# Weighted sums of the values, issued in pairs: six of the eighteen steps carry them in place of twelve

## The chip, the cores and the metric

The kernel runs on one core of a Trainium2 chip. The metric is the device time of one execution in microseconds (us), median of three runs. PE is TensorE, DVE VectorE, ACT ScalarE, POOL GpSimd, SP SyncE; PEld stands for TensorE's weight loads.

## The reference

For x of shape (4, 1024, 128), float32: a latent attention with 16 heads, a residual sum and a layer norm, a feed-forward block on weights and activations that are quantised to FP4 in blocks of 16, a residual sum and a second layer norm.

```
k_eff = (W_dq.T @ W_uq.T @ W_uk) per head;  v_eff = (W_uv.T @ W_o.T) per head
c_kv = x @ W_dkv.T;  q = x @ W_dq.T @ W_uq.T
attn = softmax(causal(q @ k_eff @ c_kv.T / sqrt(8)))
y = attn @ c_kv @ v_eff
x = layernorm(x + y)
gate, up = fp4_linear(x, w_gate), fp4_linear(x, w_up)
x = layernorm(x + fp4_linear(silu(gate) * up, w_down))
```

## The kernel before

The batch elements (4) are worked one after the other, the heads of each in four quads of four heads. A quad takes 18 steps (`STEPS`), a batch element 72 (`BODY`). In a step, PE issues in this order:

- `score_max` (L487, mask L490) for a tile 24 steps ahead: scores of which DVE takes row maxima (`maximum`, L750)
- the jobs due at this step (`misc_job`): transposes and projections in the bank `misc`, among them `yn` (L443, transposes of the attention output), `mt` (L438, the transposed maxima), and for the batch element before this one `gate` and `up` (L457), `ht` (L463), `down` (L472)
- `score_probs` (L504, mask L508) for this step's tile: transposed scores less the maxima, which ACT turns into probabilities (`exps`, L675), written to `probs`, six buffers in turn
- the calls of `weigh` (L524) due at this step

A call of `weigh` multiplies 128 keys of one half of the queries by the values: for each of the four heads an accumulating float32 matmul with a 128 x 32 weight block and 128, 256, 384 or 512 columns of `probs`, each head on its own 32 columns of the array, all into the bank `yt_ps`. The profile shows two matmuls for each, so eight a call. A quad has 12 calls (`W_LIST`, numbered 0 to 11; 0 to 3 are for the first half of the queries, 4 to 11 for the second). Their columns are 512, 384, 128, 256, then five times 512, then 384, 128, 256. The last tile that each needs is of step 1, 3, 3, 4, 6, 8, 10, 12, 14, 16, 16, 17. `W_STEP` gives the step in whose end PE issues each; a step of 18 or 19 is step 0 or 1 of the next quad.

Scores lie in three double banks `ring`, taken in turn by `score_max` and `score_probs`. So `score_probs` of a step waits for the maximum of the step before, and `score_max` for the exponentials of two steps before:

```
pe.wait_ge(t_exp.sem, pn + 1)                           # ahead of score_max
...
pe.wait_ge(s_max.sem, b * BODY + n + STEPS + LEAD)      # ahead of score_probs
```

ACT copies `yt_ps` out (`out_copy`, L683) after the exponentials of step 7 (first half) and of step 1 of the next quad (second half). DVE does in each step the maximum, then what is due: `combine` of the maxima (L759, after tile 17, in step 11), `output` (L783, L787) of a `yn` job, and pieces of the feed-forward block and of the norms. After `combine`, POOL splits the maxima in five operations (`top_split`, L986 to L994) for the job `mt` at step 13. POOL also multiplies, divides and rounds for the quantisation (L1058, L1063, L1027 to L1031). Each engine works strictly in its written order.

The feed-forward block of a batch element is worked during the attention of the next one, so quads 0 to 3 have none of it; after the last quad a closing stage does it alone.

Of the kernel before, what the change touches and what calls it, by code (L numbers as in the profile page):

```python
# [40 lines left out]
def build(nc, x, w_dq, w_uq, w_dkv, w_uk, w_uv, w_o, w_gate, w_up, w_down, out):  # L41
# [35 lines left out]
            W_LIST.append((max(t for t, _ in where.values()), c, j, where))  # L77
    W_LIST.sort(key=lambda w: w[0])
    WS = len(W_LIST)
    W_STEP = [3, 5, 6, 7, 9, 10, 12, 14, 16, 17, 18, 19]  # L80
    assert len(W_STEP) == WS and all(at > w[0] for at, w in zip(W_STEP, W_LIST))

    FREED = [max(n + 1 for n, w in enumerate(W_LIST) if t in [x for x, _ in w[3].values()]) for t in range(STEPS)]
# [50 lines left out]
    with ExitStack() as ctx:  # L134
# [259 lines left out]
        def _(pe):  # L394
# [164 lines left out]
            for b in range(B + 1):  # L559
# [3 lines left out]
                for n in range(BODY):  # L563
# [20 lines left out]

                    for w, at in enumerate(W_STEP):
                        g = n - at
# [534 lines left out]
```

## Time and profile before

| | us |
|---|---|
| median of three runs | 787.44 |
| the three runs | 787.44, 789.64, 785.46 |
| span of the profiled execution | 785.6 |

The profiled execution is known by its span, from its first to its last instruction; no other time of it is given. The profile page lists busy time by engine, a chain of work that ended last, and groups of instructions by line. The trace answers queries on a stretch of time: a timeline, the waits, and windows with the busy time of each engine. Stage by stage: the attention and feed-forward of the batch elements fill 110 to 690 us, before it lie preparation and the first maxima, after it the closing stage.

### The profile page before, as it was taken

The numbers are of one execution on the slowest core, as the hardware profiler recorded it, in microseconds if no ns is written. First come the engines' busy times: TensorE is split into PE (matmuls) and PEld (weight loads), VectorE is DVE, ScalarE is ACT, GpSimd is POOL, SyncE is SP. The second block draws the span as 40 slices with busy tenths as digits, with TensorE's granted clock in tenths as the row PEclk, the third lists the DMA queues.
The fourth block names the chain that finished last, engine by engine and source line by source line (L and its number), as shares of the span: only waits on it lengthen the run. The fifth ranks groups of instructions, "written<-read, shape, count | busy, mean of one in ns | idle before, by whom it ended". The sixth has DMA issues, their size and how long they took to land.

```text
span 785.6 us, 13071 instructions
## 1 busy us (share of the span) xinstructions
PE 661.5 (84%) x4839; PEld 328.1 (42%) x4839; DVE 589.9 (75%) x1053; ACT 393.2 (50%) x558; POOL 279.7 (36%) x402
## 2 busy tenths in 40 slices
PE   5197999999998989899898899899988997982523
PEld 2154444534443535444444445354434462441313
DVE  1287567677887979988798799978889797167871
ACT  2211566566575556565465566564656555751210
POOL 3700031000315543432236342524143344345752
PEclk9655899999999999999999999999999999995565
DMA  3462012302211032020401221011100000000000
GB/s 98 144 131 74 1 43 74 90 2 61 61 43 39 17 103 62 15 62 15 102 15 41 68 55 43 27 49 42 49 15 1 2 2 16 1 14 0 1 13 13
DMA packets 31073, 33.55 MB, mean 43 GB/s; under 512 B 5299, under 2 KB 18675, under 8 KB 31011
## 3 DMA queue, kind: packets, MB, share of 16 engines
q1 hardware_dynamic: 30099, 32.19, 14.6%
q8 instruction: 38, 0.62, 0.3%
q10 hardware_dynamic: 912, 0.54, 0.3%
q14 instruction: 24, 0.20, 0.1%
HBM read 23.84 MB, written 8.39 MB: 41 GB/s over the span
## 4 chain that ended last, share of the span: by engine, by line
PE 57%; DVE 22%; POOL 11%; issue 6%; ACT 1%; SPq 1%; DMA 1%; POOLq 0%; DVEq 0%; ACTq 0%
PE yt_ps L524 14%; PE ring L487 13%; PE ring L504 11%; DVE top L750 11%; PE ring L490 3%; PE ring L508 3%; PE misc L472 3%; PE misc L457 2%; DVE eg L860 2%; POOL hx L1029 2%; POOL hx L1027 2%; PE misc L443 1%; POOL hx L1031 1%; DVE z L817 1%; DVE hc L880 1%
## 5 line engine op out<-in xcount | busy, mean ns | idle before, releaser
L750 DVE TENSOR_REDUCE top<-ring 128x2 f32<-128x1024 f32 (+3 forms) x384 | 350.6, 941 | 101.8 <-PE ring L490 72.7
L675 ACT ACTIVATE probs<-ring 128x1024 f32<-128x1024 f32 x288 | 294.3, 1025 | 176.4 <-PE ring L508 110.9
L487 PE MATMUL ring<-k_op,q_op 72*128 72x512 bf16 (+3 forms) x768 | 209.7, 350 | 19.4 <-DMA q_op<-scratch_q 17.1
L504 PE MATMUL ring<-q_op,k_op 75*128 75x512 bf16 (+3 forms) x768 | 197.7, 332 | 13.8 <-DVE top L750 12.8
L524 PE MATMUL yt_ps<-probs,v_op 128*32 128x512 f32 (+3 forms) x1536 | 168.4, 511 | 0.3 <-ACT probs L675 0.3
L487 PEld LDWEIGHTS ring<-k_op,q_op 72*128 72x128 bf16 x768 | 69.8, 103 | 162.3 <-issue 109.8
L504 PEld LDWEIGHTS ring<-q_op,k_op 75*128 75x128 bf16 x768 | 73.3, 99 | 86.2 <-DVE top L750 35.0
L490 PE MATMUL ring<-mask_q,ident 128*128 128x128 bf16 x512 | 107.0, 230 | 0.0
L508 PE MATMUL ring<-mask_k,ident 128*128 128x128 bf16 x512 | 96.8, 224 | 0.0
L1050 POOL TENSOR_TENSOR r<-r,yq 128x128 f32<-128x128 f32 x32 | 14.5, 454 | 203.5 <-DVE yq L787 203.5
L860 DVE RECIPROCAL eg<-eg 128x118 f32<-128x118 f32 (+1 forms) x96 | 83.0, 867 | 0.0
L524 PEld LDWEIGHTS yt_ps<-probs,v_op 128*32 128x32 f32 x1536 | 30.5, 109 | 60.8 <-issue 46.3
L508 PEld LDWEIGHTS ring<-mask_k,ident 128*128 128x128 bf16 x512 | 51.4, 100 | 8.7 <-issue 5.1
L490 PEld LDWEIGHTS ring<-mask_q,ident 128*128 128x128 bf16 x512 | 53.2, 104 | 2.0
L1027 POOL TENSOR_TENSOR hx<-hx,hc 128x352 f32<-128x352 f32 x32 | 29.7, 928 | 41.8 <-DVE hc L883 41.8
L463 PE MATMUL ring<-ident,hx 128*128 128x128 f32 (+1 forms) x24 | 6.3, 394 | 34.4 <-POOL hx L1031 34.4
L986 POOL TENSOR_SCALAR top_parts<-top_all 128x32 bf16<-128x32 f32 x16 | 4.8, 297 | 76.9 <-DVE top_all L759 76.8
L1058 POOL TENSOR_TENSOR h<-gu,eg 128x352 f32<-128x352 f32 x32 | 29.6, 926 | 6.5 <-DVE eg L860 6.5
L1029 POOL TENSOR_TENSOR hx<-hx,hc 128x352 f32<-128x352 f32 x32 | 29.8, 930 | 2.5
L656 ACT ACTIVATE eg<-misc 128x352 f32<-128x352 f32 x24 | 11.1, 464 | 35.2 <-PE misc L457 35.2
L1063 POOL TENSOR_TENSOR hx<-h,h_inv 128x352 f32<-128x352 f32 x32 | 25.1, 785 | 8.9 <-DVE h_inv L875 8.7
L866 DVE TENSOR_REDUCE h_amax<-h 128x22 f32<-128x352 f32 x32 | 16.1, 504 | 14.7 <-POOL h L1058 14.6
(156 smaller groups left out, 706.1 us busy)
## 6 DMA issues: line engine op xcount, KB each, us to landing
k_op<-scratch_k SPq DMA_DIRECT2D x48, 192.0 KB
q_op<-scratch_q SPq DMA_DIRECT2D x144, 64.0 KB
scratch_q<-part SPq DMA_DIRECT2D x12, 256.0 KB, 2.4
scratch_k<-part SPq DMA_DIRECT2D x12, 256.0 KB, 2.4
xp<-in_L_attn_x_dram SPq DMA_DIRECT2D x4, 512.0 KB, 4.7
r<-in_L_attn_x_dram SPq DMA_DIRECT2D x8, 256.0 KB, 2.8
out_dram<-z SPq DMA_DIRECT2D x8, 256.0 KB, 2.3
q_op<-top_t SPq DMA_DIRECT2D x48, 8.0 KB, 1.9
```

The lines of the kernel that those rows point to most:

```text
L487: last = nc.tensor.matmul(ring[slot][:, e, at:at + n], q_op[0:ROWS, head, i * P:(i + 1) * P], k_op[0:ROWS, head, kc * CHUNK:kc * CHUNK + n ...
L490: last = nc.tensor.matmul(ring[slot][:, e, at + n - P:at + n], ident16[:, :], mask_q[:, :], start=False, stop=True)
L504: last = nc.tensor.matmul(ring[slot][:, e, at:at + n], k_op[0:rows, head, j * P:(j + 1) * P], q_op[0:rows, head, (c + 1) * CHUNK - n:(c + ...
L508: last = nc.tensor.matmul(ring[slot][:, e, at:at + P], ident16[:, :], mask_k[:, :], start=False, stop=True)
L524: last = nc.tensor.matmul(yt_ps[32 * q:32 * (q + 1), lo:CHUNK], v_op[:, j, 4 * a + q, :], probs[:, (STEPS * a + tile) % P_RING, q % 2, at: ...
L675: nc.scalar.activation(probs[:, n % P_RING, :, :], ring[(2 * n + 1) % 3][:, :, :], ACT.Exp, scale=SCALE).then_inc(t_exp.sem, 1)
L750: last = nc.vector.tensor_reduce(top[:, kc, p, :, i], ring[slot][:, :, at:at + n], AX.X, ALU.max)
L860: nc.vector.reciprocal(piece, piece).then_inc(s_v.sem, 1)
L1027: nc.gpsimd.tensor_tensor(dst, dst, magic, ALU.add).then_inc(s1.sem, 1)
L1029: nc.gpsimd.tensor_tensor(dst, dst, magic, ALU.subtract).then_inc(s2.sem, 1)
L1058: nc.gpsimd.tensor_tensor(hn.rearrange("p n k -> p (n k)"), gu[:, n, :], eg[:, n, :], ALU.mult).then_inc(h_p.sem, 1)
L1063: nc.gpsimd.tensor_tensor(hxn, hn, h_inv[:, n, :].unsqueeze(2).to_broadcast(sh), ALU.mult).then_inc(hd_p.sem, 1)
```

## The change

Only the steps of the calls move. Each call with an even number goes to the step of the call behind it, so that the calls lie two and two at steps 5, 7, 10, 14, 17 and 19.

```
-    W_STEP = [3, 5, 6, 7, 9, 10, 12, 14, 16, 17, 18, 19]
+    W_STEP = [5, 5, 7, 7, 10, 10, 14, 14, 17, 17, 19, 19]
```

## Rows read from the trace of the kernel before

**Rows 1.** The page, busy us of each engine (share of the span) x instructions.
```profile
PE 661.5 (84%) x4839; PEld 328.1 (42%) x4839; DVE 589.9 (75%) x1053; ACT 393.2 (50%) x558; POOL 279.7 (36%) x402
```

**Rows 2.** The page's groups: form, count, busy, mean ns, idle before and its releaser.
```profile
L524 PE MATMUL yt_ps<-probs,v_op 128*32 128x512 f32 (+3 forms) x1536 | 168.4, 511 | 0.3 <-ACT probs L675 0.3
```

**Rows 3.** The waits of PEld, 110 to 690 us: total us, times, longest.
```profile
PEld ring L504 <- DVE top L750: 34.2, 56, 2.2
```

**Rows 4.** Windows of quads 2, 6, 4 and 8; columns are in the first line.
```profile
core 0: us, PE busy (x) PEld busy (x) DVE busy (x) ACT busy (x) POOL busy (x), PEclk, DMA share, GB/s
146.26:179.06 32.80, 32.13 (x268) 14.33 (x265) 23.36 (x30) 19.65 (x21) 2.60 (x8) 1.00 0.13 38
299.33:340.00 40.67, 38.09 (x308) 19.70 (x306) 37.95 (x73) 23.27 (x33) 16.00 (x25) 1.00 0.13 37
212.19:254.27 42.08, 39.26 (x296) 18.52 (x293) 33.95 (x62) 25.52 (x35) 16.39 (x23) 1.00 0.13 37
376.69:423.78 47.09, 42.55 (x295) 19.42 (x293) 37.77 (x68) 25.66 (x35) 16.85 (x24) 0.93 0.24 62
```

**Rows 5.** Timeline of PE around a call (start, us), then L524 by source line.
```profile
306.81 0.22 PE L508 MATMUL ring<-mask_k,ident 128*128 128x128 bf16 x1
306.96 1.06 PE L524 MATMUL yt_ps<-probs,v_op 128*32 128x512 f32 x8
307.96 0.23 PE L487 MATMUL ring<-k_op,q_op 72*128 72x128 bf16 x1
...
L524 PEld LDWEIGHTS yt_ps<-probs,v_op x8: 106/108/109, 307.0 to 307.0; 128*32 128x32 f32 x8
L524 PE MATMUL yt_ps<-probs,v_op x8: 592/605/617, 307.0 to 307.4; 128*32 128x512 f32 x8
```

**Rows 6.** Timeline of steps 6 and 7 of quad 2.
```profile
158.12 0.61 PE L487 MATMUL ring<-k_op,q_op 72*128 72x512 bf16 x2
...
158.76 1.23 DVE L750 TENSOR_REDUCE top<-ring 128x2 f32<-128x1024 f32 x1 [0.66 <-PE ring L487]
...
159.08 0.43 PE L524 MATMUL yt_ps<-probs,v_op 128*32 128x128 f32 x8
...
160.04 0.61 PE L504 MATMUL ring<-q_op,k_op 75*128 75x512 bf16 x2
```

**Rows 7.** Windows of quad 2 by stretch: from step 2, 6, 8, 11, 15, 0.
```profile
150.55:158.12 7.57, 7.55 (x75) 4.33 (x71) 5.76 (x9) 4.79 (x6) 0.79 (x2) 1.00 0.36 106
158.12:161.15 3.03, 3.03 (x29) 0.85 (x25) 2.29 (x2) 1.83 (x3) 0.00 (x0) 1.00 0.00 0
161.15:166.82 5.67, 5.66 (x42) 2.08 (x39) 4.26 (x7) 3.97 (x5) 0.45 (x1) 1.00 0.01 3
166.82:174.28 7.46, 7.03 (x57) 2.97 (x53) 5.22 (x7) 4.36 (x6) 1.36 (x5) 1.00 0.02 3
174.28:179.99 5.71, 5.50 (x50) 2.50 (x47) 3.58 (x3) 2.86 (x4) 0.00 (x0) 1.00 0.01 3
179.99:183.35 3.36, 3.36 (x39) 1.60 (x35) 2.25 (x3) 1.84 (x3) 0.00 (x0) 1.00 0.47 135
```

**Rows 8.** Timeline of quad 2, DVE's combine and the last of POOL's five operations.
```profile
168.84 0.19 DVE L759 TENSOR_TENSOR top_all<-top 128x32 f32<-128x32 f32 x1
...
170.53 0.29 POOL L994 TENSOR_SCALAR top_parts<-top_rest 128x32 bf16<-128x32 f32 x1
```

**Rows 9.** Windows of quad 6: steps 8 to 10, steps 11 to 14.
```profile
318.16:325.82 7.66, 6.67 (x47) 2.78 (x44) 7.25 (x19) 4.78 (x10) 2.60 (x4) 1.00 0.00 1
325.82:335.23 9.41, 8.03 (x62) 3.68 (x58) 9.30 (x19) 5.55 (x8) 4.71 (x9) 1.00 0.12 32
```

**Rows 10.** Timeline of quad 6: two jobs that wait.
```profile
323.60 0.86 PE L457 MATMUL misc<-wg_t,xq_t 128*128 128x352 f32 x2 [0.99 <-DVE yq L787]
...
333.23 0.52 PE L463 MATMUL misc<-ident,hx 128*128 128x128 f32 x3 [1.20 <-POOL hx L1031]
```

**Rows 11.** Timeline of quad 8, then a window at half clock.
```profile
418.09 0.86 PE L457 MATMUL misc<-wg_t,xq_t 128*128 128x352 f32 x2 [1.96 <-DVE rest L740]
...
419.30:422.70 3.40, 3.40 (x15) 1.17 (x14) 0.60 (x2) 1.80 (x4) 2.69 (x4) 0.50 0.20 73
```

## The prediction

> **What bounds it now.** I read the page first [rows 1]: PE is busy 84% of the 785.6 us span, DVE 75%, ACT 50%. PE carries the end, but DVE is close behind. The weighted sums L524 keep PE busy 168 us [rows 2]. Next the waits of PE's loads in the steady part [rows 3] (110 to 690 us): those of `score_probs` (L504) wait 34.2 us in 56 places for a DVE maximum. So PE is the bound where a step holds much PE work, DVE where it holds little. The quads (18 steps of `BODY`) show two kinds [rows 4]: quad 2 without feed-forward work takes 32.80 us (PE 32.13, DVE 23.36 busy); quad 6 with it takes 40.67 (PE 38.09, DVE 37.95). In the second kind both engines are over 93% busy, so what counts is how evenly PE's work lies beside DVE's.
>
> **What the change does.** The same 12 calls of `weigh` per quad, 192 in all, no instruction added or removed, no DMA moved. Calls 0, 2, 4, 6, 8, 10 go to the step of the next call, so the calls lie at steps 5, 7, 10, 14, 17, 19 in pairs, and steps 3, 6, 9, 12, 16, 18 lose theirs. No new block follows directly: `exps` of step n needs the buffer of step n-6, whose call is still in a step before n in PE's order; `out_copy` at s = 7 and s = 1 waits for calls 3 and 11, which keep their steps.
>
> **The gain, per pair.** A call of 512 columns: the last score matmul starts at 306.81, the first L524 at 306.96, the next score matmul at 307.96 [rows 5]. A 128-column matmul of the mask is otherwise followed after 0.06 us in the same timeline (the granted clock is 1.00 there), so going in costs 0.15 - 0.06 = 0.09. Inside, the four matmuls of the second half start 0.45 after those of the first (307.0 to 307.4) [rows 5], so two halves are 0.91 of a slot of 1.00; coming out costs the other 0.09. A pair saves one way in and one way out if the second call follows as the second half follows the first: 0.185 us, 6 x 0.185 = 1.11 us a quad, 96 x 0.185 = 17.8 us in all. Bounds: 0.24 if the drain of the first call vanishes wholly (0.15 of fixed slot plus 0.09), nothing if the second call waits for the first to end. I take 0.185, the row of the half. The eight weight loads of a call all start at 307.0, as the first four matmuls do [rows 5], so loads do run beside matmuls here. The Trainium skill (TensorE: Matmul & The Clock Gate, Part 3) says that a weight load overlaps running matmuls only when the row group differs, and all these loads use all 128 rows. By that rule the second call's loads would lie bare; the trace does not agree within a call and has no two calls in a row. The sum by the row is -17.8 us of PE work; by the rule it is about -5 (rival 3).
>
> **The loss: how a light step runs.** `score_probs` of step n+1 needs the maximum of step n (three ring slots). In [rows 6], PE starts `score_max` of step 6 at 158.12; it takes 0.44; the maximum starts 0.20 after it, at 158.76, and takes 1.23; L504 starts 0.05 later, at 160.04. That is 1.92 from start to start. PE's own work there is 0.44 + 0.44 + 0.44 = 1.32, plus the call of step 6 (0.36 + 0.09). So PE waits 0.16 now, and will wait 0.60 without the call: the freed time is not gained. I walk each stretch from the end of one pair to the end of the next by these rules: M(n) starts when PE is free; the maximum at the later of M's end + 0.20 and DVE free, 1.23 to 1.29 long; T(n+1) at the later of PE free and that maximum's end + 0.05. Slots of M and T are 0.43 to 0.69 by start differences in the timeline; a pair costs 2.00 (512 + 512), 1.79 (512 + 384), 0.90 (128 + 256) with its way in.
>
> Quad 2, now against then [rows 7]:
> - steps 2 to 5: 7.57, then 7.37 (one wait of 0.19 for a maximum, little lost, as before)
> - 6 and 7: 3.03, then 1.92 + 0.44 + 0.90 = 3.26
> - 8 to 10: 5.67, then 5.59
> - 11 to 14: 7.46, then 7.92. Here three light steps follow each other. T12 waits 0.49 as now. Then comes the maxima transpose (`mt`, L438) at step 13: DVE's combine starts at 168.84, POOL's five operations end at 170.82 [rows 8], PE can go at +2.05. Now call 6 (1.09) covers it; then PE arrives at 3.16 after the pair's end and must wait to 4.06.
> - 15 to 17: 5.71, then 5.61
> - 0 and 1: 3.36, then 3.36
>
> The sum is 32.80 now and 33.11 then: **+0.3 us**. Savings of 1.11 are inside it; 1.4 of new waits eat them.
>
> Quad 6, the same walk with its jobs and DVE's longer extra work: steps 2 to 5 -0.29 and 6 and 7 -0.21 (jobs cover DVE there, PE never waits, the pairs' savings stay, with some rounding of slots), 8 to 10 +0.89, 11 to 14 +0.35, 15 to 17 -0.10, 0 and 1 +0.02: **+0.66 us**. The two losses:
> - 8 to 10, now 7.66 [rows 9]. The gate matmul L457 of step 10 needs the bank that DVE's `output` frees, after the maximum of step 9; it starts at 323.60 after 0.99 idle [rows 10]. DVE is the whole way there: from the stretch's start it is free at 0.48, can take maximum 8 at 0.64 and ends it at 1.87, has 1.92 of extra work (a reciprocal piece and the statistics of the second norm), ends maximum 9 at 4.98 and the output at 5.47. So L457 goes at 5.52, where it goes at 5.44 now. Call 4 (1.09) hides in that wait now; then it is paid behind it: 5.52 + 0.59 + 0.44 + 2.00 = 8.55.
> - 11 to 14, now 9.41. The transposes L463 (333.23, 1.20 idle [rows 10]) wait for POOL's chain behind the same combine (its five operations, then three of `rounded`). They go 7.41 after the stretch's start now. Then DVE comes with less behind it, the combine is 0.5 earlier, and they go at 6.88; but call 6 has left its cover and is paid after it: 6.88 + 0.33 + 0.55 + 2.00 = 9.76.
>
> The neighbours, walked alike, give +0.5 (quad 7: 11 to 14 +0.9, its step 16 gains because a pair now lies ahead of a long DVE piece) and +0.4 (quad 5: 11 to 14 +1.0, the rest gains). The mean of the three is 0.52. Sum: four plain quads x 0.3 = 1.3; eleven quads of the other kind x 0.52 = 5.7; the last quad has no `score_max`, ACT's 1.03 an exp paces its light steps: I take -0.5 (between 0 and -1.11); the last call 10 moves behind the transpose of the closing stage, at most its slot of 0.36: +0.3. Together **+6.8 us**.
>
> **The clock.** The granted clock falls to half in single windows, such as 419.3 to 422.7, right after a PE wait of 1.96 us at 418.09 [rows 11]; five such windows lie in 110 to 690. Quads 4 and 8 do the same work; quad 8, with two such windows, takes 47.09 against 42.08 [rows 4], 2.5 us a window. More and longer waits may bring more; I take one more, +2 (from -3 to +12).
>
> **Total.** The profiled execution is known by its span, 785.6 us; the three runs are 785.46 to 789.64, so what lies around the span is under their scatter. To the median 787.44 I add 6.8 + 2: **796 us**, +1.1%. What a measurement of this kernel tells from no change is about 0.5%, 3.9 us.
>
> **Rivals.**
> 1. *The switch gain comes through* (faster). PE is 84% busy and the sum of its gaps at L504 is only 34 us. If the new waits stay under 1.11 us a quad it wins; at no new wait it is -17.8, 770 us; my waits add up to 6.8 + 17.8 = 24.6, and half of them leave -5.5, 782. For it: the slots are regular to 0.01 us. Against it: the waits of [rows 6, 10] hide a call already. 0.17.
> 2. *No change*: waits and savings meet, which takes 0.4 us a quad less of waits than I found: 787. 0.18.
> 3. *The second call waits for the first* (loads not ahead). The four loads and a start, about 0.13 us of the 0.185, are lost: 96 x 0.13 = +12.5, 809 us. Against it the loads of the second half, which go ahead. 0.08. That is the rule of the Trainium skill (TensorE: Matmul & The Clock Gate, Part 3) as said.
> 4. *The clock*: waits of 2 us and more in 11 quads give six more half-clock windows: +12 with 2.0 a window, 808 us. 0.12.
> 5. My forecast, +3 to +14: 0.45.
>
> Likeliest alone: 791 to 802. Range with the others: 781 to 809. Faster 0.17, same 0.18, slower 0.65.
>
> **What would show it.** In the profile after: L524 groups of 16 with the ninth matmul 0.45 (not 0.5 or more) behind the fifth; `yt_ps` busy down by some 15 us; waits of L504 for DVE up from 34 to 60 us or more, at steps 7, 12, 13, 16; L438 waiting for POOL about 0.8 us in most quads; quads 2 and 6 at 33.1 and 41.3 us, with 11 to 14 longer and 2 to 5 shorter. If quad 2 comes out at 31.7, DVE kept up and rival 1 is right. I would be wrong if DVE's maximum starts earlier than 0.20 after M, or if the way in is not paid per pair.

## The result, and the profile after

The changed kernel takes **809.93 us** (median of four runs, 804.47 to 815.92) against 786.81 (four runs, 785.46 to 789.64): a ratio of 1.0276, 95% interval 1.0227 to 1.0325. It is slower, as forecast, but by 23 us and not by 9, and it lies just above the range (809). The profiled execution has a span of 808.3 us, against 785.6. Every ratio below leaves out three executions that ran in a slower state (two of the kernel with the last two pairs, at 954 us, and one of the kernel before, at 1571).

The page after, the lines that answer to [rows 1, 2] and [rows 4], with the granted clock in tenths by fortieths of the span (PEclk):

```profile
PE 660.6 (82%) x4839; PEld 344.6 (43%) x4839; DVE 589.8 (73%) x1053; ACT 392.6 (49%) x558; POOL 279.7 (35%) x402
...
PEclk9655899999899999999999899999989999896565
...
L524 PE MATMUL yt_ps<-probs,v_op 128*32 128x512 f32 (+3 forms) x1536 | 153.5, 519 | 0.0
```

The busy times are those of before, L524's is down from 168.4 to 153.5, and still the span is 22.7 longer: PE stands still more, and works more at half clock. PE's busy sum hides this, since a matmul at half clock counts as busy for twice as long.

Windows of quads 2, 6 and 10 after, then a stretch of 3.4 us inside quad 2 (columns as in [rows 4]); quad 10 does the same work as quad 6:

```profile
146.35:180.76 34.41, 32.48 (x268) 15.63 (x265) 23.09 (x30) 19.64 (x22) 2.60 (x8) 0.95 0.13 36
308.13:350.14 42.01, 37.30 (x308) 20.32 (x306) 37.85 (x71) 23.13 (x33) 16.32 (x25) 1.00 0.13 36
481.30:524.94 43.64, 38.93 (x308) 20.71 (x306) 37.86 (x71) 23.13 (x33) 16.33 (x25) 0.96 0.12 35
172.30:175.70 3.40, 3.40 (x22) 1.70 (x24) 1.29 (x2) 1.86 (x2) 0.00 (x0) 0.50 0.05 7
```

Quad 6 takes 42.01 where 41.33 was forecast (40.67 before). Quads 6 and 10 differ by 1.63, and the row says by what: the clock column, 1.00 against 0.96. That is one window of 3.4 us at a clock of 0.50, the 1.2 GHz level in place of 2.4 (506.8 to 510.2, inside quad 10), and 1.6 us is its price.

**Where the 22.7 us went.** I cut PE's timeline at the starts of its instructions, from the first matmul of `score_probs` in step 17, the end of quad 0, to that in step 287, the end of quad 15 (587.5 us before, 608.9 after). The shortest slot of each form (same tile, same columns, same successor) at full clock is its work; what a slot has beyond that is a wait, or, inside a half-clock window and up to the form's own length, clock. Two profiled executions of each kernel:

| us | part | work | waits | lost to the clock | time at half clock |
|---|---|---|---|---|---|
| before | 587.5 | 531.0 | 48.6 | 7.8 | 17 |
| before, again | 589.3 | 531.0 | 47.2 | 11.0 | 24 |
| changed | 608.9 | 511.7 | 74.9 | 22.4 | 48 |
| changed, again | 602.6 | 511.7 | 76.7 | 14.3 | 31 |

From the first to the first: work -19.3, waits +26.3, clock +14.6, and outside the part +1.3 (198.1 to 199.4). Together +22.9, measured 22.7. From the second to the second: -19.3 + 29.5 + 3.3 + 1.3 = +14.8, measured 14.6. Work and waits nearly repeat (waits within 2 us); the clock doesn't, and in the changed kernel it is what scatters the runs: its four have mean granted clocks of 0.904, 0.896, 0.894 and 0.884 at spans of 802.7, 808.0, 808.3 and 814.1 us.

The work: L524 in a pair of calls, after (one source line in a short stretch):

```profile
L524 PEld LDWEIGHTS yt_ps<-probs,v_op x16: 106/110/110, 321.2 to 322.1; 128*32 128x32 f32 x16
L524 PE MATMUL yt_ps<-probs,v_op x16: 486/539/617, 321.2 to 322.4; 128*32 128x512 f32 x8, 128*32 128x384 f32 x8
```

and the loads in the timeline of PEld:

```profile
321.22 0.16 PEld L524 LDWEIGHTS yt_ps<-probs,v_op 128*32 128x32 f32 x8 [0.42 <-issue]
321.68 0.13 PEld L524 LDWEIGHTS yt_ps<-probs,v_op 128*32 128x32 f32 x4 [0.30 <-issue]
```

The first eight loads are the first call's. The next four are the second call's: they start at 321.68, beside the first call's fifth to eighth matmuls, and 0.43 ahead of their own. The second call's first matmul (the ninth of the sixteen) starts at 322.107; the fifth started at 321.678, so the ninth comes 0.43 behind it. A pair of 512 and 384 columns fills 1.64 us of the timeline, where I had 1.79.

Of the waits of PE from 110 to 712 us, after, these rows (us in total, times, longest):

```profile
PE ring L504 <- DVE top L750: 14.3, 32, 1.1
PE misc L457 <- DVE yq L787: 12.4, 12, 2.1
PE misc L463 <- POOL hx L1031: 8.0, 6, 1.9
...
PE misc L438 <- POOL top_parts L994: 6.5, 10, 1.5
...
PE misc L457 <- DVE rest L740: 1.6, 2, 1.3
```

and of its loads, the first of which answers to [rows 3]:

```profile
PEld ring L504 <- DVE top L750: 33.7, 57, 1.6
...
PEld misc L457 <- DVE yq L787: 16.7, 15, 2.4
```

The same view of before has these rows, and none of a wait of L438 for POOL:

```profile
PE ring L504 <- DVE top L750: 12.8, 27, 1.7
PE misc L463 <- POOL hx L1031: 7.4, 6, 1.9
PE misc L457 <- DVE rest L740: 3.9, 2, 2.0
PE misc L457 <- DVE yq L787: 3.0, 3, 1.0
```

So the row that I had pointed at, L504 for a DVE maximum, hardly grew. What grew most is the waits of two jobs: the gate matmuls L457 for DVE's `output` (3.0 to 12.4; with those for L740, which fell, 6.9 to 14.0 in all) and `mt` (L438) for POOL (nothing to 6.5). Their timelines, in quad 2 (step 7, then `mt`) and in quad 6 (step 10, then step 14):

```profile
160.77 0.60 PE L504 MATMUL ring<-q_op,k_op 75*128 75x512 bf16 x2 [0.45 <-DVE top L750]
161.31 0.86 PE L524 MATMUL yt_ps<-probs,v_op 128*32 128x128 f32 x16
...
171.25 0.29 POOL L994 TENSOR_SCALAR top_parts<-top_rest 128x32 bf16<-128x32 f32 x1
171.69 0.23 PE L438 MATMUL misc<-ident,top_parts 128*96 128x128 bf16 x1 [0.81 <-POOL top_parts L994]
...
333.61 0.86 PE L457 MATMUL misc<-wg_t,xq_t 128*128 128x352 f32 x2 [2.08 <-DVE yq L787]
...
343.60 0.52 PE L463 MATMUL misc<-ident,hx 128*128 128x128 f32 x3 [1.22 <-POOL hx L1031]
```

At 171.69 PE has waited 0.81 for POOL's last operation; 0.6 us later, at 172.30, the half-clock window shown behind the three quads begins. In the second profile of the same kernel the same wait (0.82, at 170.99) is followed by none, and quad 2 takes 32.8.

### The profile page after: what moved, and what is told of

Read it like the earlier page. It is cut to its first block, busy times and chain, and to the rows that moved or that the text cites. A ratio compares the mean times of both kernels' runs of the same rounds, so it can differ in the third digit from the quotient of the medians.

```text
span 808.3 us, 13070 instructions
## 1 busy us (share of the span) xinstructions
PE 660.6 (82%) x4839; PEld 344.6 (43%) x4839; DVE 589.8 (73%) x1053; ACT 392.6 (49%) x558; POOL 279.7 (35%) x402
## 3 DMA queue, kind: packets, MB, share of 16 engines
q1 hardware_dynamic: 30099, 32.19, 14.3%
## 4 chain that ended last, share of the span: by engine, by line
PE 52%; DVE 28%; POOL 11%; issue 6%; ACT 1%; SPq 1%; DMA 1%; POOLq 0%; DVEq 0%; ACTq 0%
DVE top L750 15%; PE yt_ps L524 15%; PE ring L487 11%; PE ring L504 10%; PE misc L457 3%; DVE eg L860 3%; PE misc L472 3%; PE ring L490 2%; PE ring L508 2%; POOL hx L1029 1%; POOL hx L1027 1%; POOL hx L1031 1%; DVE hc L880 1%; DVE rest L740 1%; PE misc L443 1%
## 5 line engine op out<-in xcount | busy, mean ns | idle before, releaser
L487 PE MATMUL ring<-k_op,q_op 72*128 72x512 bf16 (+3 forms) x768 | 211.4, 352 | 21.1 <-DMA q_op<-scratch_q 17.8
L504 PE MATMUL ring<-q_op,k_op 75*128 75x512 bf16 (+3 forms) x768 | 202.3, 339 | 15.3 <-DVE top L750 14.3
L524 PE MATMUL yt_ps<-probs,v_op 128*32 128x512 f32 (+3 forms) x1536 | 153.5, 519 | 0.0
L487 PEld LDWEIGHTS ring<-k_op,q_op 72*128 72x128 bf16 x768 | 73.6, 104 | 121.9 <-ACT probs L675 42.8
L504 PEld LDWEIGHTS ring<-q_op,k_op 75*128 75x128 bf16 x768 | 74.8, 101 | 85.7 <-DVE top L750 34.9
L490 PE MATMUL ring<-mask_q,ident 128*128 128x128 bf16 x512 | 109.1, 234 | 0.0
L1050 POOL TENSOR_TENSOR r<-r,yq 128x128 f32<-128x128 f32 x32 | 14.6, 455 | 215.8 <-DVE yq L787 215.8
L524 PEld LDWEIGHTS yt_ps<-probs,v_op 128*32 128x32 f32 x1536 | 40.0, 113 | 78.2 <-issue 70.4
L463 PE MATMUL ring<-ident,hx 128*128 128x128 f32 (+1 forms) x24 | 6.3, 393 | 34.5 <-POOL hx L1031 34.5
L457 PE MATMUL misc<-wg_t,xq_t 128*128 128x352 f32 x48 | 22.8, 559 | 14.0 <-DVE yq L787 12.4
L866 DVE TENSOR_REDUCE h_amax<-h 128x22 f32<-128x352 f32 x32 | 16.2, 505 | 14.8 <-POOL h L1058 14.8
```

The costliest lines, as they stand in the source:

```text
L457: nc.tensor.matmul(to[:, 0:FF], xq_t[:, k * P:(k + 1) * P], w[:, :], start=True, stop=True).then_inc(s.sem, 1)
L487: last = nc.tensor.matmul(ring[slot][:, e, at:at + n], q_op[0:ROWS, head, i * P:(i + 1) * P], k_op[0:ROWS, head, kc * CHUNK:kc * CHUNK + n ...
L490: last = nc.tensor.matmul(ring[slot][:, e, at + n - P:at + n], ident16[:, :], mask_q[:, :], start=False, stop=True)
L504: last = nc.tensor.matmul(ring[slot][:, e, at:at + n], k_op[0:rows, head, j * P:(j + 1) * P], q_op[0:rows, head, (c + 1) * CHUNK - n:(c + ...
L524: last = nc.tensor.matmul(yt_ps[32 * q:32 * (q + 1), lo:CHUNK], v_op[:, j, 4 * a + q, :], probs[:, (STEPS * a + tile) % P_RING, q % 2, at: ...
```

## The experiments

Each was timed beside the kernel before on the same chip, whose median was 787.1 to 788.3 us; "over before" is the difference of the two medians. "The profile" of a run is that of one execution, which need not be its median one.

### Which pairs cost: one back, and one alone

```
changed    W_STEP = [5, 5, 7, 7, 10, 10, 14, 14, 17, 17, 19, 19]
six_back   W_STEP = [5, 5, 7, 7, 10, 10, 12, 14, 17, 17, 19, 19]
four_back  W_STEP = [5, 5, 7, 7, 9, 10, 14, 14, 17, 17, 19, 19]
only_six   W_STEP = [3, 5, 6, 7, 9, 10, 14, 14, 16, 17, 18, 19]
only_four  W_STEP = [3, 5, 6, 7, 10, 10, 12, 14, 16, 17, 18, 19]
```

> Five pairs stay, call 6 goes back from step 14 to step 12. Theory A (place): the pair at 14 is bad because call 6 covered the waits of the jobs at steps 13 and 14; the walk gives 0.5 to 1.0 us a quad back, so about 10 us with fewer half-clock windows: 800 us. Theory B (even share): each of the six pairs carries a sixth of the 22.7 us: 806 us. Theory C (clock by chance of the schedule): the time follows the number of half-clock windows and not the place: anything from 800 to 812, with waits unchanged but for L438.

> Only calls 6 and 7 are paired (step 14), all others as in the kernel before. Theory A: mt (L438) and ht (L463) waits come, some +8 to +12 us: 795 to 799. Theory B: +3.8, 791. If the switch gain dominated: -3.7, 783.

> Five pairs stay, call 4 goes back from step 10 to step 9, where it covers DVE's output ahead of the gate job. Theory A: the wait of L457 for yq falls by about 12 us in all, and 8 us of time come back: 802 us. Theory B: 806 us.

> Only calls 4 and 5 are paired (step 10). Theory A: the gate job's wait for yq grows in the feed-forward quads, +0.9 us each less the pair's 0.23 saving in the plain ones: +5 to +8, 792 to 795. Theory B: +3.8, 791.

Measured: call 6 back at step 12: 805.11, 1.0210 (1.0176 to 1.0245). Only call 6 moved: 805.96, 1.0232 (1.0202 to 1.0261). Call 4 back at step 9: 806.92, 1.0233 (1.0201 to 1.0266). Only call 4 moved: 799.89, 1.0156 (1.0120 to 1.0192).

One moved call of six, call 6, costs +18.4 us by itself, nearly as much as all six; call 4 by itself +12.3. Yet taking either back out of the six gives 3 to 5 us, which the scatter of the changed kernel (804 to 816) doesn't tell from nothing. By themselves these two runs look like theory B (806 for both); the single moves rule an even share out, since it would be 3.8 each. So the loss is neither an even share per pair nor a sum of single costs. The waits of PE with only call 6 moved show the wait that the prediction named (L438 for POOL, at step 13):

```profile
PE ring L504 <- DVE top L750: 13.0, 25, 1.7
PE misc L463 <- POOL hx L1031: 8.1, 6, 1.9
PE misc L438 <- POOL top_parts L994: 7.5, 10, 1.5
```

and with only call 4 moved it is the other one:

```profile
PE misc L457 <- DVE yq L787: 9.4, 6, 2.1
```

### The pairs that should cost nothing

```
three_pairs     W_STEP = [5, 5, 6, 7, 9, 10, 12, 14, 17, 17, 19, 19]
last_two_pairs  W_STEP = [3, 5, 6, 7, 9, 10, 12, 14, 17, 17, 19, 19]
```

> Pairs only at steps 5, 17 and 19; calls 2, 4 and 6 keep their steps 6, 9 and 12, where they cover a wait. By PE's account the three pairs save 48 x 0.2 = 10 us of work; the new waits are 0.25 us at step 1 and, in the quads with feed-forward work, 0.8 at step 4 (the gate job), some 5 to 8 us. Theory place: 784 to 790, about as before. Theory half clock follows any wait of 0.7 us and more: 792 to 798.

> Pairs only at steps 17 and 19. Saving 32 x 0.2 = 6.5 us of PE work, new waits of 0.25 us at step 1 alone, too short to matter for the clock: 781 to 787, the only version that may come out faster than the kernel before. If crowding by itself costs: 789 or more.

> The kernel before once more, for a second profile: 17 us of half clock and 8 us lost by it in the first one. If the clock term differs between the kernels and not only between executions, it stays under 12 us.

> The changed kernel once more, for a second profile: PE work and waits as in the first one within 2 us (512 and 75), clock loss between 15 and 28 us.

Measured: three pairs 794.34, 1.0076 (1.0052 to 1.0101). The last two pairs 788.62, 0.9993 (0.9975 to 1.0011): no difference. The kernel before, built again: 788.42, 0.9997 (0.9976 to 1.0017). The change again: 806.67 in two runs, 1.0229 (1.0177 to 1.0281).

So calls 8 and 10 move for nothing, and call 0 costs +6 - 0 = about 6 us (by difference; it wasn't moved alone). With three pairs the gate matmul of step 4 waits 0.60 us in four quads, and its waits of before have none at this step. The account of PE's timeline, made as above (differences to before: profiled part, work, waits, clock; one profile each), shows where single costs don't add up:

| us | part | work | waits | clock |
|---|---|---|---|---|
| only call 4 moved | +16.5 | -3.0 | +8.6 | +11.0 |
| only call 6 moved | +20.5 | -2.3 | +10.1 | +12.8 |
| calls 0, 8, 10 moved | +3.7 | -10.4 | +7.6 | +6.6 |
| sum of the three | +40.7 | -15.7 | +26.3 | +30.4 |
| changed (call 2 too) | +21.4 | -19.3 | +26.3 | +14.6 |
| changed, call 6 back | +18.4 | -16.9 | +17.7 | +17.6 |
| changed, call 4 back | +19.3 | -16.7 | +19.0 | +17.0 |

Work and waits do add up (the missing 3.6 of work is near call 2's 16 pairs at 0.235 = 3.8). The clock doesn't: each of these kernels loses 7 to 18 us more to it than the kernel before, whether it has one pair or six. Putting call 6 or 4 back takes 7 to 9 us of waits away, and the clock's loss doesn't fall with them.

One profile says little about the clock, as the two of the changed kernel show (+14.6 and +3.3). Every execution has a mean granted clock, though, and it gives an estimate of the half-clock time: 2 x (1 - clock) x span. For the profiled execution of the changed kernel that is 171 us, 48 of them in the part and the rest before and behind it. In the four profiles above, 1 us of half clock lost 0.46 us. With the means over all executions of a kernel, against those of the kernel before beside them:

| us over before | half clock | x 0.46 | work + waits | sum | measured (means) |
|---|---|---|---|---|---|
| changed, 6 executions | +26 | +12 | +9 | +21 | +21 |
| only call 4 moved | +26 | +12 | +6 | +17 | +12 |
| only call 6 moved | +21 | +9.5 | +7.8 | +17 | +18 |
| calls 0, 8, 10 moved | +18 | +8.4 | -2.8 | +6 | +6 |
| calls 8, 10 moved | +6 | +2.6 | -2.9 | 0 | 0 |
| POOL late by four (below) | +18 | +8.2 | +7.8 | +16 | +17 |
| POOL late by two (below) | +15 | +7.0 | +3.2 | +10 | +9 |

The sums meet the measured times within 2 us but for the kernel with only call 4 moved, whose times don't follow its clocks either (805.80 us at 0.896, 798.92 at 0.893). So some 12 us of the changed kernel's loss are the clock's, by this estimate.

### Waits without any move

Four operations of POOL whose result nobody reads stand ahead of the last one of the split of the maxima. Together they take 1.03 us. No call moves, the calls stay as before; only POOL is late. Then two of them in place of four.

```
             nc.gpsimd.tensor_tensor(...)                      # L992
+            for _ in range(4):                                # late_by_two: range(2)
+                nc.gpsimd.tensor_scalar(top_late[:, _, :], t, -1.0, None, ALU.mult)
             nc.gpsimd.tensor_scalar(...)                      # L994, here L997
```

> The kernel before, all calls in their old steps, but POOL does four more small operations (into a buffer that nothing reads) ahead of the last one of the maxima's split, so that L438 comes 1.2 us later and PE waits about 1 us at step 13 of each quad, as with the pair at 14. If a bare wait of 1 us costs what e2_only_six lost, the time is 800 to 806, with 40 us or more of half clock in the attention part. If only the wait itself costs and is partly made up for: 790 to 795, half clock as before (17 us).

> The kernel before with two extra POOL operations ahead of the last one of the maxima's split (four gave waits of 0.85 us at step 13 and +16 us). Two make L438 wait about 0.35 us. If a wait costs its own length and no more: at most +5, 793. If what counts is a wait long enough to start half-clock windows: about +2, 790, with half clock as before (17 to 24 us). If the POOL work as such costs: +8, half of the four.

Measured: four operations 804.59, 1.0214 (1.0174 to 1.0255); two 798.23, 1.0122 (1.0086 to 1.0157). The waits of PE with four (lines are one to three further down than before):

```profile
PE ring L505 <- DVE top L751: 13.8, 27, 1.7
PE misc L464 <- POOL hx L1034: 7.8, 6, 1.4
PE misc L439 <- POOL top_parts L997: 7.6, 10, 1.5
```

These are nearly the rows of the kernel with only call 6 moved (7.6 and 7.5 for `mt`), and the times are near too (804.6 and 806.0). Taking the cover off `mt` and making POOL late cost the same. In the account: waits +7.8, clock +18.6 (its profiled execution was the slowest of six, span 810.9; the others have 800.4 to 806.0 at clocks of 0.906 to 0.898 and so lose less). Waits of 7.6 us in ten places thus cost 16 us. With two operations, waits +3.2 and clock +4.2 of the profile make the +7.3 of its part, while the medians say +11: the profiled execution was the second shortest of its six, and over all six the clock's part is about 7 (table above). The +11 met none of the three expectations (at most +5, +2, +8); it is nearest to "the POOL work as such", and no run adds POOL work that delays nobody. That the table's sum closes without such a term speaks against it, no more.

Which quads pay is seen in the windows of its quads; these are 6 and 7 with four operations:

```profile
303.21:346.44 43.23, 39.84 (x309) 19.89 (x307) 37.96 (x73) 23.28 (x33) 17.00 (x29) 0.96 0.13 35
346.44:383.13 36.69, 35.42 (x298) 17.64 (x296) 30.87 (x63) 20.52 (x25) 14.59 (x26) 1.00 0.16 41
```

Quad 2 pays its wait, 33.40 in place of 32.80. Quad 6 pays 2.56 (40.67 before): a wait and, by its clock of 0.96, a window. Quad 7 (36.69 before) pays nothing.

### Moving the waiting job

If `mt` waits for POOL at step 13, let it be issued at step 14, a step later.

```
-    jobs += [(STEPS * a + 13, "mt", (a + 1) // QUADS, (a + 1) % QUADS) for a in range(QUADS)]
+    jobs += [(STEPS * a + 14, "mt", (a + 1) // QUADS, (a + 1) % QUADS) for a in range(QUADS)]
```

with all six calls moved, with only call 6 moved, and with POOL late and no call moved:

> All six pairs as in the change, and the job mt moved from step 13 to step 14. If the wait of L438 for POOL's split (0.5 to 1.2 us in nearly every quad) is what pairing 6 and 7 costs, directly and by the half-clock windows that it starts, this gives about 10 us back: 800. If the empty step 12 as such costs (DVE's pace), nothing comes back: 810.

> Only calls 6 and 7 paired, as in e2_only_six (+18), with the job mt moved to step 14. If the wait in front of L438 is what that one pair costs, directly and through the clock: 786 to 792. If the empty step 12 and the crowded step 14 cost by themselves: 800 or more.

> The kernel before with the four extra POOL operations and the job mt moved from step 13 to step 14: POOL is as late as in e7_late_maxima, but the call at step 12 and the tile of step 13 cover it on PE. If PE's wait in front of L438 is the cause of the +16, nearly all comes back: 788 to 793. If POOL's lateness is (through the transposes L463 at step 14): 800 and more.

Measured: six calls moved 805.01, 1.0207 (1.0177 to 1.0238); only call 6 803.58, 1.0193 (1.0160 to 1.0226); POOL late 804.88, 1.0238 (1.0193 to 1.0283). In all three the wait of `mt` is gone or nearly gone, and the time hardly moves (-5, -2, 0; the -5 is within the scatter of the changed kernel). So the wait of `mt` in itself is not the cause that I had expected it to be: take it away, and another takes its place. With call 6 moved, its wait went to the next in line: L504 waits 20.9 us for DVE's maxima, where it waited 13.0, since step 12 still has no call.

```profile
PE ring L504 <- DVE top L750: 20.9, 36, 1.7
```

With POOL late it went to the transposes L464 (L463 before), whose operand comes from POOL after the same split:

```profile
PE misc L464 <- POOL hx L1034: 12.9, 6, 2.5
...
PE misc L439 <- POOL top_parts L997: 0.8, 1, 0.8
```

This last kernel is the cleanest look at the clock, since many quads are untouched. The window of its quad 6:

```profile
305.60:348.82 43.22, 39.69 (x309) 19.94 (x307) 37.52 (x73) 23.14 (x33) 15.68 (x27) 0.96 0.13 35
```

Quad 2 is at its 32.80 of before and quad 7 at 36.70 (36.69 before). Quad 6 takes 2.55 more. The timeline of its step 14, and the windows ahead of and behind that wait:

```profile
340.50 0.60 PE L464 MATMUL misc<-ident,hx 128*128 128x128 f32 x3 [2.14 <-POOL hx L1034]
```

```profile
336.40:340.80 4.40, 2.26 (x24) 1.64 (x22) 4.40 (x8) 1.17 (x2) 4.24 (x9) 1.00 0.02 3
340.80:344.20 3.40, 3.40 (x15) 0.79 (x14) 0.68 (x1) 1.56 (x3) 1.22 (x2) 0.50 0.04 8
```

The same transposes waited 1.20 us before [rows 10], and the clock stayed at 1.00 behind them. Here they wait 2.14, and 0.3 us after they start a half-clock window begins. 0.94 of more wait and 1.6 of a window are the 2.55.

Six quads (5, 6, 9, 10, 13, 14) have this wait, and their counts over the kernels show the clock's loss growing with it. Before, in both profiles, five of the six waits are 1.04 to 1.20 us, and none has a window begin near it; the sixth, 1.9, has one 0.8 us behind. That 1.9 in quad 14 stands in eleven profiles of these kernels, and in all of them a window begins within 1.2 us of its end. In this kernel all six are 2.03 to 2.52, and all six have one, begun between 0.6 us ahead of the wait's end and 1.3 us behind it. With four POOL operations and `mt` at step 13 they are 1.29 to 1.37, after a wait of 0.56 to 1.50 of `mt` some 2.8 us earlier, and five of six have one, all within 0.6 us of the wait's end. The length of this one wait isn't all of it: with two operations five of them are 1.29 to 1.30 and three have a window, with only call 6 moved five are 1.22 to 1.24 and two have one.

### Filling the waits

To see whether PE's standing still brings the half clock, filler matmuls of 512 columns (repeats of a score matmul into a free slot of `ring`) are put ahead of the longest waits, sized to them by each kernel's profile.

```
+FILL = {0: 6, 16: 5, 18: 4, 32: 2, 46: 4, 50: 3, 70: 1}                                # before
+FILL = {0: 4, 10: 2, 13: 1, 16: 3, 18: 4, 31: 1, 32: 3, 46: 7, 49: 1, 50: 3, 67: 1}    # changed
+    for _ in range(FILL.get(n, 0) if b > 0 else 0):
+        if _ == 0:
+            pe.wait_ge(t_exp.sem, b * BODY + n)
+        nc.tensor.matmul(ring[(2 * n + 2) % 3][:, 0, :], q_op[0:ROWS, 4 * na, 0:P],
+                         k_op[0:ROWS, 4 * na, 0:CHUNK], start=True, stop=True)
```

> The kernel before with matmuls that only fill its longest PE waits: a repeat of a score matmul of 512 columns into the ring slot that is free, its result overwritten by the next tile: 25 for each of three batch elements. Theory clock (an idle PE starts the half-clock windows): half-clock time in the attention part falls from 17 us to under 7, time 780 to 785. Theory waits alone: nothing to gain, the fillers cost up to 3 us: 787 to 791.

> The change with such fillers in its long waits (steps 0, 10, 14, 16 of quads with feed-forward work, 30 matmuls for each of three batch elements). Theory clock: half-clock time falls from 48 us to 25 or less and 8 us come back: 802. Theory waits alone: 810 to 813.

Measured: before with fillers 793.48, 1.0056 (1.0036 to 1.0075); changed with fillers 808.23, 1.0258 (1.0209 to 1.0308). The changed kernel's half-clock time in the part fell from 48 and 31 us in its two profiles to 24, but the fillers are 19.7 us of work and the waits fell by 12.9, from 74.9 to 62.0, so a third of them filled no wait. The median is 1.7 us below the changed kernel's, within the scatter, and this doesn't decide how much of the loss is the clock's. By the mean clocks of its six executions it has 15 us more half clock than the kernel before, where the changed one has 26: about 5 us won, against 6.8 of fillers that filled nothing. In the kernel before, 17 us of half clock became 20, where "under 7" was expected if idle time starts the windows, and the fillers cost 5.4 us. Waits alone don't account for the windows that the kernel before has.

## Why the forecast was too low, point by point

**The pair's gain: right, slightly too small.** Forecast 0.185 us a pair, 17.8 in all; the account gives 19.3. The ninth matmul starts 0.43 behind the fifth (forecast 0.45), and a pair's slot is 1.64 for 512 and 384 columns and 1.86 for twice 512 (forecast 1.79 and 2.00 with the way in, of which I took 0.09 as the way in's; so 1.70 and 1.91 without). Where both parts are found the saving is 0.235 (0.14 between the calls, 0.09 of the way in), my upper bound: the drain of the first call vanishes. Over all 96 pairs the account gives 0.20 each.

**Rival 3 fell.** The second call's loads run beside the first call's matmuls, although all use 128 rows; rival 3's 0.13 us a pair was not paid. By the rule of the Trainium skill (TensorE: Matmul & The Clock Gate, Part 3), taken for row groups alone, they should have lain bare. The trace does not agree.

**The waits: right in sum, off in place.** Forecast 24.6 us (6.8 + 17.8), measured 26.3 and 29.5. In quad 2 the walk held: L504 of step 7 waits 0.62 by the slots of the account (its row says 0.45), where I had 0.60; `mt` waits 0.97 (row: 0.81), where I had 0.90. A plain quad at full clock takes 32.8 (quad 2 of the second profile), where I had 33.1 (in the first it takes 34.41 with its window). In quad 6 the stretches are:

```profile
313.29:322.87 9.58, 8.97 (x82) 5.48 (x78) 9.22 (x18) 6.54 (x11) 3.43 (x5) 1.00 0.28 73
322.87:328.17 5.30, 5.30 (x52) 3.91 (x48) 4.50 (x6) 1.70 (x2) 1.65 (x3) 1.00 0.01 3
328.17:336.69 8.52, 6.44 (x47) 2.92 (x44) 7.89 (x22) 5.42 (x10) 2.60 (x4) 1.00 0.00 1
336.69:346.46 9.77, 8.04 (x63) 3.85 (x59) 8.53 (x16) 4.85 (x7) 5.52 (x10) 1.00 0.11 31
346.46:351.93 5.47, 5.26 (x50) 2.51 (x46) 4.80 (x8) 3.07 (x3) 1.38 (x3) 1.00 0.07 17
```

Steps 8 to 10 take 8.52 (forecast 8.55), 11 to 14 take 9.77 (9.76), 15 to 17 take 5.47 (5.61). The miss is steps 2 to 5: 9.58, where I had 8.70. I had written that jobs cover DVE there and PE never waits. But the gate matmul L457 of step 4 too waits for DVE's `output`, 0.77 us, and call 0 at step 3 had covered it. That is +0.9 in each quad with such a gate wait at step 4 (quads 6, 10, 13 and 14), and with the clock's part on top the likely source of the 6 us of call 0 in the experiments. My forecast for L504 (34 us to 60 or more) was wrong in place: the jobs stand ahead of `score_probs` in PE's order and take the wait first.

**The step that failed: the clock.** I wrote "More and longer waits may bring more; I take one more, +2 (from -3 to +12)". In place of +2 the two pairs of profiles show +14.6 and +3.3 (half-clock time of 17 and 24 us before, 48 and 31 after), and the estimate over all executions is +12. By the first pair: clock 12.6 more than forecast, waits 1.7 more (step 4's gates, partly made good elsewhere), outside 1.0 more, the pairs 1.5 better; 13.8 together, the distance from 796 to 810. The mechanism of rival 4 held: "waits of 2 us and more in 11 quads give six more half-clock windows", 808 us. Its price of 2.0 to 2.5 a window was too high (1.6), its count too low (9 more windows of 3.4 us in the first profile), so that 6 x 2.0 = 12 came near 9 x 1.6 = 14 partly by luck. Its condition was too narrow: windows also come behind waits of about 1 us, as at 171.69. I gave it 0.12.

**What the experiments show of the cause.** A wait of the same size put in by a late POOL, without any move, costs the same (804.6), and two pairs that uncover no job's wait cost nothing (788.6). So the loss isn't in how the pairs run; it is in what the moved calls no longer cover: `mt` and whatever waits next if `mt` does not (call 6), the gate of step 10 (call 4), the gate of step 4 (call 0). For call 6 one rival is not excluded: that the empty step 12 costs by itself, through DVE's pace, as the expectation with `mt` at step 14 put it (800 or more; measured 803.6). The last two pairs uncover nothing of the kind and cost nothing, but gain nothing either: -6.9 of work in the account, +4.0 of waits, +5.1 of clock.

**Left open.** What exactly starts a window. Of the waits of over 2 us, some are followed by one (506.78, 2.25 us in the slots' account, window at 506.83), while the same wait in quad 6 (333.61) is not; with only call 4 moved the same wait has a window about 1 us behind it in all three quads. And in the changed kernel a window at 288.4 has no wait of 0.7 us in the 24 us before it. That the clock's part is some 12 us rests on the estimate from the mean clocks; the fillers, meant to show it directly, cost as much as they gave back. A kernel with pairs that keeps a call ahead of each of the three waits wasn't tried with more than two pairs; none of the versions run beats the kernel before.

## What to carry to other kernels

On an engine that works in order, a block of work ahead of a wait is worth its whole length, up to the wait; before moving it, look up for each thing issued between its old and its new place what that thing waits for, jobs as much as the main chain. Moving the waiting thing itself one step later didn't help: the next consumer of a late engine took the wait. And where a forecast adds waits of 1 to 2 us to a busy TensorE, price them at twice their length or more (here 16 us for 7.6, and some 10 for 3.2), since the clock's loss came on top. It did not grow with the number of causes: one moved call lost about as much to the clock as six.

## What the hardware showed beyond that

- The half-clock stretches of the attention part last 3.4, 6.8 or 10.2 us, and one of 3.4 costs 1.6 us in a quad of the second kind (42.01 and 43.64, the same work).
- The transposes L463 of the six quads: waits of 1.04 to 1.23 us (two profiles each of before and changed, five of six) left the clock at full, those of 2.03 to 2.52 with POOL late all had a half-clock window begin within 1.3 us of their end. With POOL late by four operations at 1.29 to 1.37, `mt`'s wait ahead of them, it was five of six; with only call 6 moved, at 1.22 to 1.24, two of five.
- Two accumulating calls in a row, four column strips of 32 each, save 0.235 us against the same calls with score matmuls between them, way in included.
- The four times of the kernel before spread over 4 us, those of the changed one over 11, and the latter follow the mean granted clock. With POOL late by four operations they spread over 10. The times of the kernel before, 785 to 792 us in all series at clocks of 0.906 to 0.913, follow it only weakly.
